# Spreading the softmax reciprocals through DRAM instead of through TensorE in a cross-attention kernel

## What is computed

```python
qh = (q @ Wq + bq);  kh = (k @ Wk + bk);  vh = (v @ Wv + bv)          # 16 heads of 64
attn = einsum('bqhd,bkhd->hbqk', qh, kh) * mask
attn = exp(attn - max(attn)) * mask                                    # one maximum over everything
attn = attn / (sum(attn, axis=-1) + 1e-15)
out = einsum('hbqk,bkhd->bqhd', attn, vh).reshape(Bn, Tq, 1024) @ Wo + bo
x = out + residual
result = (x - mean) / sqrt(var + 1e-5) * gamma + beta
```

## Time and profile before

| | before |
|---|---|
| median of 3 runs | 1731.38 us |
| profiled execution | 1729.62 us |
| its span | 1727.8 us |
| PE busy | 1666.0 us (96%) |
| DVE busy | 1157.9 us (67%) |
| ACT busy | 945.0 us (55%) |
| POOL busy | 419.0 us (24%) |
| moved by DMA | 315.01 MB, 182 GB/s over the span |
| second phase | from about 912 us, 32 units |

### The profile page before, as it was taken

One profiled execution on the slowest core, in us unless ns is written; L12 is line 12 of the kernel. 1 busy time (PEld: TensorE's weight loads), 2 busy tenths in 40 slices (PEclk: granted clock), 3 DMA queues, 4 the chain that ended last, 5 costly groups with the idle time before them and its releaser, 6 DMA issues. The chain is left out here.

```text
span 1727.8 us, 31110 instructions
## 1 busy us (share of the span) xinstructions
PE 1666.0 (96%) x11011; PEld 848.1 (49%) x11012; DVE 1157.9 (67%) x2362; ACT 945.0 (55%) x1417; POOL 419.0 (24%) x519
## 2 busy tenths in 40 slices
PE   4999999999999999999995999999999999999997
PEld 4435556465464654645542444444444444444443
DVE  7665555665556655566545887878787877887774
ACT  7755555555545555455544555555564556555542
POOL 0000000000000000000000555555555555555556
PEclk8999999999999999999997999999999999999999
DMA  7455354452644526445236456655655456555621
GB/s 232 147 200 172 119 211 161 161 188 103 225 147 175 188 84 243 140 172 193 74 146 223 159 199 243 231 215 193 234 223 190 190 221 243 218 209 204 243 107 65
DMA packets 81469, 315.01 MB, mean 182 GB/s; under 512 B 5392, under 2 KB 9616, under 8 KB 71696
## 3 DMA queue, kind: packets, MB, share of 16 engines
q1 hardware_dynamic: 81424, 314.41, 49.7%
HBM read 184.37 MB, written 130.02 MB: 182 GB/s over the span
## 5 line engine op out<-in xcount | busy, mean ns | idle before, releaser
L70 PE MATMUL ps_s<-x_hi,g_hi 128*128 128x512 f16 x1024 | 389.7, 381 | 7.5 <-ACT s L509 7.4
L72 PE MATMUL ps_s<-x_hi,g_lo 128*128 128x512 f16 x1024 | 389.3, 380 | 0.0
L71 PE MATMUL ps_s<-x_lo,g_hi 128*128 128x512 f16 x1024 | 389.3, 380 | 0.0
L79 PE MATMUL ps_o<-u,p_hi 128*128 128x512 f16 x1024 | 388.4, 379 | 0.0
L80 PE MATMUL ps_o<-u,p_hi 128*128 128x512 f16 x1024 | 388.1, 379 | 0.0
L81 PE MATMUL ps_o<-u,p_lo 128*128 128x512 f16 x1024 | 388.1, 379 | 0.0
L509 ACT ACTIVATE s<-ps_s,c_bias 128x512 f32<-128x512 f32 x256 | 176.0, 688 | 309.5 <-PE ps_s L72 306.3
L631 DVE TENSOR_TENSOR score_max<-score_max,tile_max 128x1 f32<-128x1 f32 x257 | 40.8, 159 | 315.6 <-ACT s L509 313.8
L898 ACT ACTIVATE p_hi<-ps_bc 128x512 f16<-128x512 f32 x256 | 149.4, 593 | 176.9 <-DVE ps_bc L988 174.9
L1079 POOL PARTITION_ALL_REDUCE key_max<-score_max x1 | 0.4, 377 | 917.0 <-issue 917.0
L1099 POOL TENSOR_TENSOR y<-y,gamma_b 128x512 f32<-128x512 f32 x128 | 162.8, 1272 | 192.6 <-ACT y L908 192.6
(11 more groups left out here) (87 smaller groups left out, 2367.9 us busy)
## 6 DMA issues: line engine op xcount, KB each, us to landing
scores<-s SPq DMA_DIRECT2D x30, 2048.0 KB, 7.6
s<-scores SPq DMA_DIRECT2D x30, 2048.0 KB, 7.8
x<-xT_in SPq DMA_DIRECT2D x32, 1024.0 KB, 9.5
u_halves<-u_out SPq DMA_DIRECT2D x64, 512.0 KB, 3.0
u<-u_halves SPq DMA_DIRECT2D x16, 2048.0 KB, 11.8
y<-x_in SPq DMA_DIRECT2D x32, 1024.0 KB, 10.2
out<-y SPq DMA_DIRECT2D x31, 1024.0 KB, 4.2
mask<-maskT_in SPq DMA_DIRECT2D x32, 256.0 KB, 10.4
```

The costliest lines, as they stand in the source:

```text
L70: pe.matmul(out, lhs_hi, rhs_hi, start=first, stop=False)
L71: pe.matmul(out, lhs_hi, rhs_lo, start=False, stop=False)
L72: return pe.matmul(out, lhs_lo, rhs_hi, start=False, stop=last)
L79: pe.matmul(out, lhs_hi, rhs_hi, start=False, stop=False, skip_group_check=True)
```

## The change

The reciprocals no longer pass through PE. The eight sums stand once, as 4h + p in each 32 rows; sel_sum now carries 1/1024 in place of 1, and the tiny term is put in the bank by ACT before the sums (tiny), so PE adds to it. DVE inverts from the bank to SBUF (r32). SP stores the reciprocals in a DRAM tensor r_d with four small transfers (store_r), waits for them, and loads them again, each head's row read 64 times, into r_bc, 128 x (8 x 512) float32, with four transfers of 64 partitions and 8 KB rows (spread_r). DVE multiplies scores and r_bc, both in SBUF, into one of three banks ps_p. Two more units of scores fit in s_more, so scores are loaded four units ahead; exponentials, sums, reciprocals and their spreading happen three units ahead. The sums stand at (2, 4). The shift of the norm is made by POOL, with one operation more for minus the mean. SP's order in a unit begins with the store of the output.

```diff
-        part = sb("part", [P, 2])
-        den = sb("den", [P, HT])
-        r_hi, r_mid, r_all = sb("r_hi", [P, HT], BF16), sb("r_mid", [P, HT], BF16), sb("r_all", [P, 2, HT], BF16)
+        s_more = sb("s_more", [P, 2, NP, TT])
+        r32 = sb("r32", [P, 2, HT])
+        r_bc = sb("r_bc", [P, 2, NP, TT])
-        sums_at = (1, 7)
+        sums_at = (2, 4)
...
+            def store_r(n, u):
+                sp.wait_ge(r_done, n + 1)
+                for q in range(4):
+                    th, a = q // 2, q % 2
+                    sp.dma_start(r_d[u % UNITS, :, 4 * a:4 * a + 4, th * HT:(th + 1) * HT],
+                                 r32[32 * q:32 * q + NP, u % 2, :]).then_inc(r_stored, 16)
+            def spread_r(n, u):
+                sp.wait_ge(r_stored, 64 * n + 64)
...
+                for k in range(2):
+                    for h in range(2):
+                        rows = r_d[u % UNITS, h:h + 1, 4 * k:4 * k + 4, :].rearrange("a p t -> a (p t)")
+                        sp.dma_start(r_bc[rows_of(h), u % 2, 4 * k:4 * k + 4, :].rearrange("r p t -> r (p t)"),
+                                     rows.to_broadcast([NK, 4 * TT])).then_inc(bc_in[u % 2][k], 16)
...
             sp.dma_start(sel_sum[:, :, :], sel_sum_d).then_inc(sum_in, 16)
-            sp.dma_start(part[:, :], part_d).then_inc(sum_in, 16)
+            load_scores(2, 2)
+            load_scores(3, 3)
             load_u(0, B - 1)
...
+            for n in range(2):
+                store_r(n, n)
+                spread_r(n, n)
+            store_r(2, 2)
             def group(g, first, last):
                 for u in range(UNITS):
+                    if not (first and u == 0):
+                        store_y(g, u - 1)
+                    if not last:
+                        load_scores(n + UNITS, u)
                     if not (last and u >= UNITS - 2):
-                        load_scores(g * UNITS + u + 2, u)
                         load_x(g, u + 2)
                     if u % UB == 0 and not (last and u == UB):
...
                         load_u(1 - u // UB, g * GB + u // UB)
-                    if not (first and u == 0):
-                        store_y(g, u - 1)
+                    if not (last and u >= UNITS - 3):
+                        if first and u == 0:
+                            spread_r(2, 2)
+                        store_r(n + 3, u + 3)
+                        spread_r(n + 3, u + 3)
...
-                        if more and (t, p) in spread_at:
-                            spread(n + 1, 1 - s, spread_at[t, p])
-                        if more2 and (t, p) == sums_at:
-                            sums(n + 2, s)
+                        if more3 and (t, p) == sums_at:
+                            sums(n + 3, u + 3)
...
+            def tiny(n):
+                    act.wait_ge(r_done, n)
+                act.activation(ps_sum[:, 0:HT], zeros[:, :], ACT.Identity, bias=tiny_sum[:, :]).then_inc(tiny_filled, 1)
...
                     halves(0, 1)
-                    if more2:
-                        exps(n + 2, u, 0)
-                    halves(2)
-                    if more2:
-                        exps(n + 2, u, 1)
-                    halves(3)
+                    if more3:
+                        tiny(n + 3)
+                        exps(n + 3, u + 3, 0)
+                    halves(2, 3)
                     if more:
                         fill(n + 1, 0)
                     norm(g, u, 0)
+                    if more3:
+                        exps(n + 3, u + 3, 1)
                     halves(4, 5)
...
+                dve.reciprocal(r32[:, u % 2, :], ps_sum[:, 0:HT]).then_inc(r_done, 1)
+            def scale_p(n, u, p):
+                s = u % 2
+                if p % 4 == 0:
+                    dve.wait_ge(bc_in[s][p // 4], 16 * n - 16 * s + 32)
...
+                dve.tensor_tensor(ps_p[p % RBANKS][:, :], scores_of(u)[:, p, :], r_bc[:, s, p, :], ALU.mult)\
+                   .then_inc(p_scaled, 1)
...
                     scale(7)
                     split(6)
+                    if more3:
+                        invert(n + 2, u + 3)
                     residual(g, u, 2)
...
+                pool.tensor_tensor(less_mean[:, t:t + 1], mean_var[:, t, 0:1], minus_one[:, :], ALU.mult)
                 pool.wait_ge(eps_added, k)
                 pool.tensor_tensor(rstd[:, t:t + 1], var_eps[:, t:t + 1], minus_half[:, :], ALU.pow)\
                     .then_inc(rstd_done, 1)
+                pool.wait_ge(rstd_done, k)
+                pool.tensor_tensor(shift[:, t:t + 1], less_mean[:, t:t + 1], rstd[:, t:t + 1], ALU.mult)\
+                    .then_inc(shift_done, 1)
```

More of the change, by code:

```diff
@@ L709, in output_phase @@
         minus_half, ln_eps = sb("minus_half", [P, 1]), sb("ln_eps", [P, 1])
+        less_mean, minus_one = sb("less_mean", [P, TB]), sb("minus_one", [P, 1])
+        zeros, tiny_sum = sb("zeros", [P, HT]), sb("tiny_sum", [P, 1])
         ps_sum = bank("ps_sum")
-        r32, rest = ps_sum[:, HT:2 * HT], ps_sum[:, 0:HT]
-        ps_bc = [bank(f"ps_bc{i}") for i in range(RBANKS)]
+        ps_p = [bank(f"ps_p{i}") for i in range(RBANKS)]
         ps_o = [bank(f"ps_o{i}") for i in range(OBANKS)]
@@ L720, in output_phase @@
             "key_max_done", "max_local", "max_global", "max_done"))
-        s_in = [sem(f"s_in{i}") for i in range(2)]
+        s_in = [sem(f"s_in{i}") for i in range(UNITS)]
         u_in = [sem(f"u_in{i}") for i in range(2)]
@@ L808, in _, with sums @@
             pe.sem_inc(o_summed, 2 * TB)
-            def sums(n, s):
-                if not (isinstance(n, int) and n == 0):
-                    pe.wait_ge(r_all_done, n)
+            def sums(n, u):
+                pe.wait_ge(tiny_filled, n + 1)
                 for i in range(4):
@@ L820, in sums @@
                         mm = pe.matmul(ps_sum[32 * q:32 * q + 32, 0:HT], sel_sum[:, i, :],
-                                       s32[:, s, p, th * HT:(th + 1) * HT],
-                                       start=(i == 0), stop=(i == 3), skip_group_check=True)
+                                       scores_of(u)[:, p, th * HT:(th + 1) * HT],
+                                       start=False, stop=False, skip_group_check=True)
                 mm.then_inc(e_summed, 1)
[L825 to L834, removed]
             def unit(g, u, last):
                 n, s, b = g * UNITS + u, u % 2, u // UB
-                more, more2 = not (last and u == UNITS - 1), not (last and u >= UNITS - 2)
+                more3 = not (last and u >= UNITS - 3)
                 if u % UB == 0:
@@ L859, in group @@
                     unit(g, u, last)
-            for o in ps_o:
-                mm = pe.matmul(o[:, :], sel_bc[:, 0, 0, :], sel_bc[:, 0:2, :, :].rearrange("r p t k -> r (p t k)"),
-                               start=True, stop=True)
+            pe.wait_ge(u_in[0], 16)
+            for o in (*ps_o, ps_sum):
+                mm = pe.matmul(o[:, :], u2[:, 0, 0, 0, 0:P], u2[:, 0, 0, 0, :], start=True, stop=True)
             mm.then_inc(o_written, 1)
[L866 to L870, removed]
+            pe.wait_ge(sum_in, 16)
+            for n in range(3):
+                sums(n, n)
             with pe.Fori(0, NG - 1) as g:
@@ L881, in exps @@
                 if not isinstance(n, int) or n >= UB:
[L882 to L883 removed]
+                    act.wait_ge(s_in[u % UNITS], 4 * n - 4 * (u % UNITS) + (16 if u % UNITS >= UB else 0))
+                e = scores_of(u).rearrange("r (a b) t -> r a b t", a=2)[:, :, 2 * half:2 * half + 2, :]
                 act.activation(e, e, ACT.Exp, bias=neg_max[:, 0:1]).then_inc(exp_done, 1)
[L886 to L892, removed]
+            def tiny(n):
+                if not (isinstance(n, int) and n == 0):
+                    act.wait_ge(r_done, n)
+                act.activation(ps_sum[:, 0:HT], zeros[:, :], ACT.Identity, bias=tiny_sum[:, :]).then_inc(tiny_filled, 1)
             def round_p(n, s, p):
@@ L1019, in group @@
                     n, s = g * UNITS + u + 1, (u + 1) % 2
-                    more, more2 = not (last and u == UNITS - 1), not (last and u >= UNITS - 2)
-                    scale = lambda p: scale_p(n, s, p) if more else None
+                    more, more3 = not (last and u == UNITS - 1), not (last and u >= UNITS - 3)
+                    scale = lambda p: scale_p(n, u + 1, p) if more else None
                     split = lambda p: split_p(n, s, p) if more else None
@@ L1059, in _ @@
             dve.tensor_scalar(neg_max[:, :], key_max[:, :], -1.0, None, ALU.mult).then_inc(max_done, 1)
-            dve.wait_ge(sum_in, 32)
-            invert(0)
-            second_part(0)
-            third_part(0, 0)
+            for n in range(3):
+                invert(n, n)
             for p in range(NP):
```

160 lines of the change are left out of this document (57 added, 103 removed).

## The result

| | before | after |
|---|---|---|
| median of 7 runs, us | 1731.6 | **1738.39** (1736.22 to 1740.13) |
| after over before | | 1.0042 (95%: 1.003 to 1.0053) |
| profiled execution and its span, us | 1729.6, 1727.8 | 1738.4, 1736.5 |
| moved by DMA, MB | 315 | 382 |

The changed kernel is 0.4% **slower**. I had forecast 1717, faster; the range of 1676 to 1768 holds the result, the direction is wrong.

A forecast was written before the change was run, and what follows sets the result against it. PE bounds the kernel before; after, the DMA queue mildly, 24.4 us a unit against PE's 22.7. Sum: 1729.6 - 53.6 - 2.0 + 11 + 32 = 1717 us, range 1676 to 1768 for 8 in 10.

The forecast's parts named there:

- PE's saving: PE in the second half: spreading products gone, 53.6 us, unit 24.4 to 22.7; one set of sums leaves the loop, 2.0.
- The prologue: Start of the second phase: unit 0 effectively 9.3 us later, second spread 1.6 more, together 11 us lost.
- scale_p … 2.3 us: DVE's scale reading two SBUF tiles: collisions with POOL add 2.3 us a unit, DVE at 19.6 under 22.7, costing nothing.
- no change that anything waits for: Norm's shift: coming from POOL two short steps after rstd instead of by hand-over to DVE, costing nothing.
- at most 17.5 of 22.7: POOL's busy time per unit with eight added one-column operations, 1.5 to 4.4 us on 13.1.
- DVE is held by POOL: Rival, chance 0.06: from 5.4 us of collisions a unit DVE is the bound; over 1800 us at the upper end.
- 26 x 1.7 - 12 = 32 us lost: Units 3 to 28: queue 1.7 us a unit longer than PE over 26 periods, less 12 us of lead.
- 13.0 + 3.0 + 8.4 = 24.4 us: DMA queue's period per unit: existing transfers, idle gap at the store, spreading at 250 GB/s; PE needs 22.7.
- the constants' 254 GB/s: Prologue's broadcast constants, taken as nearest to reading one 8 KB row 64 times: spreading would take 8.3 us.
- 12 us before it is needed: Stock of the queue: unit 4's first half of the spread reciprocals lands some 12 us early.
- a DMA share of 0.85 to 0.9: Sign in a middle stretch that the queue is the bound; 0.75 if PE is.
- SP's waits end with DVE's reciprocal rather than the store: Sign that the forecast is wrong, read from what ends SP's waits in the queue; no size given.

The follow-up runs named there:

- run 5: Changed kernel with scale_p's second operand its own bank (reciprocals left out) and spreading loads cut to one pair of four: 1686.87 us, 0.9747 of before.
- run 2: Changed kernel with scale_p multiplying by its own bank's old content instead of r_bc, all loads kept: 1738.37 us, 1.0047 of before.
- run 1: Changed kernel with spreading loads of one pair instead of four, scale_p multiplying by the neighbouring pair's scores in SBUF: 1735.72 us, 1.0031 of before.
- run 7: Changed kernel, result complete, with ACT's norms of blocks 0, 1 and 3 placed later: 1737.17 us, 1.0041 of before.
- run 10: Changed kernel, division left out, spreading by two 1 MB loads to 128 partitions, head 0's row for both heads: 1736.5 us, one execution.
- run 9: Changed kernel with only SP's order changed, x loaded between the reciprocals' store and the wait for it: 1737.41 us, 1.0039 of before.
- run 8: Changed kernel with norms later and x loaded between the reciprocals' store and its wait, result complete: 1688.90 us, 0.9756 of before.
- run 3: Changed kernel with the norm's shift back on DVE and POOL's two added operations gone: 1740.05 us, 1.0054 of before.
- run 6: Changed kernel with shift on DVE and spreading loads of one pair of four, scale_p multiplying by the neighbouring pair: 1736.56 us, 1.0033 of before.
- run 12: Run 8 with scores 3 and x 1 loaded behind the first spreading in the prologue: 1689.89 us, 0.9766 of before.

## Why the prediction was wrong

**PE's saving: right.** Unit 22.7 (22.69 in run 5), clock full; one set of sums out of the loop.

**The prologue: right to a microsecond, by luck in part.** I put unit 0 effectively at 951.6. PE starts it at 950.42, runs nine products some 0.43 us apart at the lower clock (granted 0.57 from 950 to 954; 1.7 us lost) and waits four more times (1.75), so effectively 953.9; against 942.3 that is 11.6 us, where 11 were forecast. Here is the luck: I had missed that the first phase ends 5.3 us earlier (the load of sel_sum is issued at 906.54, before at 911.81), and the start of the phase took more than that back.

**"scale_p … 2.3 us": size right, price wrong.** 8 x 0.24 = 1.9 us a unit (913 and 953 against 692; the bank operand of run 2 gives 684). The Trainium skill, "SBUF — State Buffer", "Who interferes with whom", has the two engines exclude each other in this case; the trace agrees, since two operands in SBUF collide whichever tile they are (912 to 945 ns in run 1), one in the bank does not (684 in run 2), and neither do two while POOL is idle (0.69 us). But I priced it by DVE's busy time, "19.6, under 22.7, so it costs nothing at that size", and left POOL's side out.

**The step that failed: "no change that anything waits for", and "at most 17.5 of 22.7".** Busy shares (POOL 17.1, DVE 19.6 of 24.37 after) fit beside PE. The loop DVE, POOL, ACT, DVE doesn't: its half turns add up to 24.38. The step from POOL to ACT that I put at nothing is the longest wait of all, 122.3 us in 16.4 units. I walked the loop only once, for the exponentials of one unit, and never round to the p_hi on which DVE waits. An engine that executes in order adds its waits to the loop, and busy shares leave them out. The collisions lengthen this loop by at least 2.6 us of 24.4 in the turn read above (1.9 in the half shown, 0.7 in beta and var_eps of the other), which would leave 21.8, under PE's 22.7; run 5 bears that out, with units of 22.69 and the collisions gone. The rival "DVE is held by POOL" asked for 5.4 us of collisions; it took half of that, in the loop.

**The second step that failed: "26 x 1.7 - 12 = 32 us lost". The queue's period was right, its stock wrong, its effect hidden.** I put 13.0 + 3.0 + 8.4 = 24.4 us. Measured where the queue is the bound: 24.74 in run 2, 24.70 in run 7, long and short units in turn as forecast. The stock was to last to about unit 9; in run 2 PE's sums leave their 22.69 us after unit 4 (1061.53). In the changed kernel the time from the store's issue to the spreading's grows from 9.3 to 11.7 us over 20 units, 0.12 a unit, so there it would be 24.49. The rate was 225 to 236 GB/s, not 250. That the constants' 254 GB/s gave the same price was chance: run 10 shows no limit by the repeated row of 8 KB, and what slows those rows of 2 KB stays open. The Trainium skill, "SBUF — State Buffer", "Door 1: The DMA port swizzle", gives 196 for 1 MiB; the direction agrees, the size is the measurement's. "12 us before it is needed" counted only r_bc; run 2 shows the exponentials waiting for the scores instead, which stand in the same queue and have less slack. With the loop opened runs 2 and 7 still take 1738.4 and 1737.2, so this step alone would have turned the direction, as the loop alone does in runs 1 and 9 (1735.7, 1737.4). So the term of 32 should have been about 52 for either wall: 31 x (24.37 - 22.7). With it the sum is 1729.6 - 53.6 - 2.0 + 11.6 + 51.8 = 1737.4, against 1738.4 measured in that execution.

**What would show it.** The sign that I put ahead of all, a DMA share of 0.85 to 0.9, came (0.93) and pointed at the wrong wall. "I am wrong if … SP's waits end with DVE's reciprocal rather than the store" was half the right sign: from 1000 to 1650 us SP waits 204.6 us for the reciprocal and 234.1 for the store, in run 2 53.7 and 361.5. The better ones were that units with and without a load of u were alike, and that DVE waits for r_bc only 5.0 us in the whole run.

**Open:** how much of the loop each collision is worth, and whether the loop has another tight place behind the one that run 7 loosened. Nor is it known how long the loop is with the norms later and a free queue, since in run 8 the queue is the next bound. Loading the reciprocals by one transfer over 128 partitions with each head's own row wasn't tried.

## What to carry to other kernels

When a change moves work between in-order engines, follow one full turn of the waits (each engine's instruction, what stands ahead of it, who waits for it) back to where it began and compare its length with the bound; busy shares under 100% prove nothing. When a single undoing gives nothing, look in its profile at who waits now, and take away both suspects together: here two walls of 24.4 and 24.7 us a unit made every single edit look useless, and removing the pair gave 3%. In a queue that stores and then loads the same data back, put a load that nobody needs yet between the store and its wait.

## What the runs showed of the hardware

- Loads of 512 KB to 64 partitions, four in a row, moved 225 to 236 GB/s at a full busy share (1.02 to 1.04); loads to 128 partitions moved 393 to 426, of 512 KB too (404). One 8 KB row read 128 times cost little or nothing (393, at a share of 0.93).
- A DVE multiplication with both operands in SBUF beside POOL's elementwise work took 912 to 1136 ns on average over runs 1, 7, 8 and the changed kernel, instead of 684 to 692, and POOL paid as well: in the changed kernel 1520 instead of 1269 ns for beta (512 columns), 389 instead of 190 for var_eps (one column). Short instructions suffered most in proportion, and they sat in the loop.
- Loop and queue differ in the units' pattern: 24.36 to 24.38 twenty times in a row in the changed kernel, 22 to 24 and 25 to 28 in turn where the queue was the bound (runs 2 and 7). With the shift on DVE (runs 3 and 6) the loop too was uneven, 24.1 with a 25.6 among them, so the pattern alone decides nothing.
- After standing 3.93 us, and 1.45 more between the halves of the sums, PE ran at a granted clock of 0.50 until 975 (run 12): 4.1 us lost by the clock on top of 5.4 of standing.
